# Graph attention layer on one core: the transposed node one-hots are compared by GpSimd instead of turned on TensorE

## The reference

```python
feats = jnp.maximum(x @ w1 + bb1, 0.0) @ w2 + bb2
x_cat = jnp.concatenate([feats[row], feats[col], elem[:, None]], axis=1)
hid = jnp.maximum(x_cat @ a1 + aab1, 0.0)
e1 = (hid @ a2 + aab2)[:, 0]
e1 = jax.nn.leaky_relu(e1, negative_slope=0.2)
w = jnp.exp(e1 - jnp.max(e1))
pooled = jax.ops.segment_sum(w[:, None] * feats[col], row, num_segments=n)
row_sum = jax.ops.segment_sum(w, row, num_segments=n) + 1e-10
return pooled / row_sum[:, None]
```

## Time and profile before

| what | value |
|---|---|
| time, median of 3 executions | 4831.8 us (4830.55 to 4842.57) |
| profiled execution, span from its first to its last instruction | 4828.3 us |
| busy, share of the span | TensorE 88%, VectorE 92%, ScalarE 79%, GpSimd 56% |
| tile loop | from about 1556 us to about 4690 us |

### The profile page before, as it was taken

One profiled execution on the slowest core, in us unless ns is written; L12 is line 12 of the kernel. 1 busy time (PEld: TensorE's weight loads), 2 busy tenths in 40 slices (PEclk: granted clock), 3 DMA queues, 4 the chain that ended last, 5 costly groups with the idle time before them and its releaser, 6 DMA issues.

```text
span 4828.3 us, 133194 instructions
## 1 busy us (share of the span) xinstructions
PE 4260.4 (88%) x24114; PEld 3004.1 (62%) x24115; DVE 4460.2 (92%) x25378; ACT 3835.5 (79%) x12983; POOL 2693.5 (56%) x2886
## 2 busy tenths in 40 slices
PE   1598998898896999999999999999999999999990
PEld 1355555555555777777777777777777777777760
DVE  8799999999996999999999999999999999999998
ACT  1587778778774888888888888888888888888884
POOL 5366666666664555555555555555555555555544
PEclk9999999999997999999999999999999999999995
DMA  2133333333334877777777777777777777777757
GB/s 85 43 73 86 79 71 80 81 77 80 79 76 137 240 225 221 228 225 224 224 225 224 225 225 221 226 224 224 225 224 224 224 225 225 225 225 225 221 172 212
DMA packets 266918, 851.82 MB, mean 176 GB/s; under 512 B 107916, under 2 KB 109584, under 8 KB 266861
## 3 DMA queue, kind: packets, MB, share of 16 engines
q0 software_dynamic: 169920, 673.54, 50.0%
q1 hardware_dynamic: 63543, 160.18, 11.2%
q10 hardware_dynamic: 33398, 17.49, 1.4%
HBM read 739.10 MB, written 111.90 MB: 176 GB/s over the span
## 4 chain that ended last, share of the span: by engine, by line
PE 36%; ACT 27%; issue 3%; DVE 2%; DMA 1%; ACTq 0%; POOL 0%; DVEq 0%; SPq 0%; POOLq 0%
ACT z L1164 18%; PE psum L971 15%; PE psum L975 9%; PE psum L958 8%; ACT onehot L1193 3%; ACT onehot_t L1182 3%; PE psum L984 3%; ACT onehot L1197 2%; PE psum L939 1%; DVE z L1689 1%; DVE z L1682 0%; PE psum L995 0%; ACT onehot L1195 0%; DVE z L1705 0%; DMA p_win<-p_table 0%
## 5 line engine op out<-in xcount | busy, mean ns | idle before, releaser
L754 POOL DMA_INDIRECT z<-qf_table,rec x1664 | 1609.2, 967 | 1454.9 <-PE psum L958 1027.1
L1164 ACT ACTIVATE z<-z 128x64 f32<-128x64 f32 x6656 | 1651.1, 335 | 0.0
L971 PE MATMUL psum<-p_win,onehot_t 128*128 x9984 | 1407.8, 274 | 84.1 <-ACT onehot_t L1182 68.3
L971 PEld LDWEIGHTS psum<-p_win,onehot_t 128*128 128x128 bf16 x9984 | 966.8, 97 | 540.0 <-issue 214.4
L958 PE MATMUL psum<-z,onehot 128*128 128x260 f32 x3328 | 1029.4, 391 | 6.7 <-DVE acc L1617 4.9
L975 PE MATMUL psum<-z,ident 128*128 128x258 f32 x3328 | 1002.7, 383 | 0.0
L1568 DVE SCALAR_TENSOR_TENSOR z<-z,a_b 128x129 f32<-128x129 f32 x3328 | 884.3, 290 | 5.6 <-issue 0.2
L1568 DVE SCALAR_TENSOR_TENSOR z<-psum,a_b 128x129 f32<-128x129 f32 x3328 | 828.2, 286 | 0.0
L1558 DVE TENSOR_TENSOR z<-z,psum 128x258 f32<-128x258 f32 x1664 | 698.6, 420 | 94.6 <-PE psum L975 90.6
L1617 DVE TENSOR_TENSOR acc<-acc,psum 125x260 f32 x1664 | 702.3, 422 | 25.3 <-PE psum L958 2.4
L695 POOL DMA_INDIRECT sorted_rows<-z x300 | 478.5, 1595 | 403.9 <-DVE z L1447 321.6
(11 more groups left out here) (220 smaller groups left out, 5576.3 us busy)
## 6 DMA issues: line engine op xcount, KB each, us to landing
p_table<-acc SPq DMA_DIRECT2D x100, 338.6 KB
p_win<-p_table SPq DMA_DIRECT2D x100, 338.6 KB
z<-qf_table,rec POOLq DMA_INDIRECT x1664, 4.5
qf_table<-acc SPq DMA_DIRECT2D x75, 339.5 KB
acc<-in_x_dram SPq DMA_DIRECT2D x25, 448.0 KB
z<-in_x_dram SPq DMA_DIRECT2D x20, 560.0 KB
out_dram<-z ACTq DMA_DIRECT2D x20, 560.0 KB
qf_table<-z SPq DMA_DIRECT2D x25, 339.5 KB
```

Source lines behind the costliest of these rows:

```text
L754: pool.indirect_dma_start(out=z_t[:, o + j, :], out_offset=None, in_=qf_table, in_offset=bass.IndirectOffsetOnAxis(ap=rec[:, o + j, 3:4].b ...
L971: mm = pe.matmul(to, onehot_t[:, j, :], p_flat[:, bass.ds((w % 2) * (3 * ZW) + (part * ZW + o), n)], start=(part == 0), stop=(part == 2 an ...
L1164: op = act.activation(z_t[:, slot, o:o + DO], z_t[:, slot, o:o + DO], ACT.Copy, scale=z_t[:, slot, o + DO:o + HF])
```

## The change

The transposed one-hots no longer come from the others. In the stage that makes the records, GpSimd also takes the row numbers and the three weight parts of each group as bf16 (`rows_b`), and SyncE writes them to `edge_rows` in device memory. In the tile loop ScalarE starts three transfers for each group of four tiles (`load_nodes`): the 512 row numbers go to all of partitions 0 to 124 (as 112 and 13 partitions), and the three weight parts to partitions 125 to 127 of `onehot_t`, which now has three halves. GpSimd then compares 125 x 512 of them in place with each partition's number (`match_nodes`). `turn`, `take_turned` and the copy of the weight parts are gone. ScalarE makes the f32 one-hots, which only `sum_up` still reads, a step later. Some semaphores are merged, and two constants move in SBUF.

```diff
+    HALVES = 3
...
+        node_id = sb("node_id", [P, 1])
-        onehot_t = sb("onehot_t", [P, SB, P], BF16)
+        onehot_t = sb("onehot_t", [P, HALVES, SB // 2, P], BF16)
...
             for g in range(BULK):
+                sp.wait_ge(s_rows_b, g + 1)
+                sp.dma_start(rows_t[g * P:(g + 1) * P, :, :], rows_b[:, g % 2, :, :]).then_inc(s_rows_st[g % 2], 16)
                 sp.wait_ge(s_field_a, g + 1)
...
+            for g in range(BULK):
+                pool.wait_ge(s_stage[g % 4], g // 4 * 16 + 16)
+                if g >= 2:
+                    pool.wait_ge(s_rows_st[g % 2], g // 2 * 16)
+                of = stage[:, g % 4, :].rearrange("p (s f) -> p f s", f=NF)
+                pool.tensor_copy(rows_b[:, g % 2, 0, :], of[:, 0, :])
+                pool.tensor_copy(rows_b[:, g % 2, 1:4, :], of[:, 3:6, :]).then_inc(s_rows_b, 1)
...
+                def match_nodes(off, u):
+
+                    h = (k + off) * 2 + u
+                    pool.wait_ge(s_oht_ld[h % HALVES], (i * 2 + h // HALVES) * 48 + 48)
+                    pool.sem_inc(s_passed, 1)
+                    own = onehot_t[0:WN, h % HALVES, :, :].rearrange("p t n -> p (t n)")
+                    pool.tensor_scalar(own, own, node_id[0:WN, :], None, ALU.is_equal).then_inc(s_oht, 1)
+
                 for j in range(SB):
                     if live(i, k, 1):
                         gather(j)
+                    if j == 1 and live(i, k, 0):
+                        match_nodes(0, 1)
+                    if j == 5 and live(i, k, 1):
+                        match_nodes(1, 0)
...
-                def turn(off, u):
-
-                    group = (i * SPB + (k + off)) * 2 + u
-                    pe.wait_ge(s_onehot, group + 1)
-                    since(pe, s_oht, group)
-                    for j in range(HALF_SB):
-                        mm = pe.transpose(psum[:, 6, j * P:(j + 1) * P], onehot[:, ((k + off) * SB + u * HALF_SB + j) % RING, :], ident[:, :])
-                    mm.then_inc(s_oht_mm, 1)
...
-                    act.activation(onehot_t[:, u * HALF_SB:(u + 1) * HALF_SB, :].rearrange("p t n -> p (t n)"),
-                                   psum[:, 6, 0:HALF_SB * P], ACT.Copy).then_inc(s_oht, 1)
...
-                    act.activation(onehot[:, oo:oo + HALF_SB, WN:P], rec_b[:, oo:oo + HALF_SB, 2:5], ACT.Copy)
...
+                def load_nodes(off, u):
+
+                    h = (k + off) * 2 + u
+                    own = onehot_t[:, h % HALVES, :, :].rearrange("p t n -> p (t n)")
+                    at = bass.ds((i * SPB + (k + off)) * (SB * P) + u * (HALF_SB * P), HALF_SB * P)
+                    if live(i, k, off - 2 + u):
+                        act.wait_ge(s_z_mm, tile(off - 2 + u, (1 - u) * HALF_SB + HALF_SB - 1) + 2)
+                    for a, b in ROWS:
+                        act.dma_start(own[a:b, :], edge_rows[0:1, at].to_broadcast([b - a, HALF_SB * P])).then_inc(s_oht_ld[h % HALVES], 16)
+                    act.dma_start(own[WN:P, :], edge_rows[1:4, at]).then_inc(s_oht_ld[h % HALVES], 16)
...
+                if live(i, k, 1):
+                    load_nodes(1, 0)
                 if live(i, k, 0):
-                    take_turned(0, 1)
-                if live(i, k, 1):
-                    onehots(1, 0)
+                    onehots(0, 0)
...
-                    if j == 0 and live(i, k, 1):
-                        take_turned(1, 0)
                     if j == SB // 2 and live(i, k, 1):
-                        onehots(1, 1)
+                        load_nodes(1, 1)
+                    if j == SB // 2 and live(i, k, 0):
+                        onehots(0, 1)
```

More of the change, by code:

```diff
@@ L85, in gnn_layer @@
     records = nc.dram_tensor("records", (P * NT, 4), F32, kind="Internal").ap()
+    edge_rows = nc.dram_tensor("edge_rows", (4, NT * P), BF16, kind="Internal").ap()
     base_rows_d = nc.dram_tensor("base_rows", (BLOCKS, 2, CB * W), BF16, kind="Internal").ap()
@@ L324, in gnn_layer @@
         s_onehot = sem("s_onehot")
-        s_oht_mm = sem("s_oht_mm")
+        s_rows_b = sem("s_rows_b")
+        s_rows_st = [sem(f"s_rows_st{n}") for n in range(2)]
+        s_oht_ld = [sem(f"s_oht_ld{n}") for n in range(HALVES)]
         s_oht = sem("s_oht")
@@ L580, in _ @@
             sp.wait_ge(s_rec_st, 16 * BULK)
+            for n in range(2):
+                sp.wait_ge(s_rows_st[n], (BULK + 1 - n) // 2 * 16)
             sp.dma_start(rec[:, 0:SB, :].rearrange("p t n -> p (t n)"), rec_d[:, 0:SB * 4]).then_inc(s_rec[0], 16)
@@ L970, in hidden_src @@
                         for part in range(3):
[L971 removed]
+                            mm = pe.matmul(to, onehot_t[:, (k * 2 + j // HALF_SB) % HALVES, j % HALF_SB, :], p_flat[:, bass.ds((w % 2) * (3 * ZW) + (part * ZW + o), n)],
                                            start=(part == 0), stop=(part == 2 and not (o and PEH)), skip_group_check=True)
@@ L1005, in step @@
                         hidden_src(j)
-                    if j == SB // 4 and live(i, k, 0):
-                        turn(0, 1)
                     if j == SB // 4 and live(i, k, -1):
@@ L1011, in step @@
                         max_to_all()
-                    if j == SB - SB // 4 and live(i, k, 1):
-                        turn(1, 0)
                     if j % 4 == 3 and j < SB - 1 and live(i, k, 0):
```

86 lines of the change are left out of this document (40 added, 46 removed).

## The result

The changed kernel takes 4928.15 us in the median of four executions (4925.22 to 4934.23), the kernel before 4831.18 (4830.36 to 4842.57). The ratio is 1.0198, with an interval of 1.0184 to 1.0213: slower by 97 us, where 73 us less was forecast. The profiled execution of the changed kernel has a span of 4932.4 us and was the slowest of the four (4934.23 as timed).

What follows compares the result with a forecast made beforehand. TensorE bounds now, VectorE after the change: 14.28 + 0.43 = 14.71 us a step, 0.38 less; 208 x 0.38 = 79, less 6, is 73 us faster: 4759 from the median, range 4680 to 4950.

Steps and rivals of the forecast that it cites:

- M: Time of one GpSimd compare of 125 x 512: 0.87 us taken, 0.62 at the least, 2.50 at the most.
- GpSimd's own time does not matter: GpSimd's queue in the tile loop: 8.2 us a step plus 1.7, said not to matter; only the effect on VectorE would.
- TensorE stops being the bound: Tile loop: TensorE falls to 13.98 us at most, VectorE's 14.13 plus 0.15 idle gives 14.28 a step without new cost.
- break-even of 1.15: Compare length in us above which holding VectorE eats the 0.78 us gain left after the start's 6 us.
- VectorE held until GpSimd's instruction is done: Tile loop: the skill's exclusive port lock holds VectorE's two-SBUF-input products for GpSimd's whole instruction; price 0.43 us a step.
- the rival that had this M (1.6): VectorE held longer than it gains, in tiles 1 and 6: 1.68 us, 15.96 a step, 5019; 27 in 100.
- Where the compares fall: Compares miss VectorE's products for 1.08 us behind the sixth gather (no cost), 0.44 behind the second (price 0.43 us).
- my 4.24 us: Time from the start of tile j - 2 to the compare behind gather j: 0.76 + 1.10 + 1.42 + 0.96.
- ScalarE 13.7 us a step: ScalarE: 12.88 less 1.17 plus 2.0 for six transfer starts; rival that it becomes the bound, 4834, 10 in 100.
- the DMA: Rival: row numbers land late and the compare holds gathers; half a microsecond a step gives 4863; 5 in 100.
- Once, +6 us: Outside the steps: 1 us for record-stage casts and stores, about 5 us later first TensorE product at the loop's start.
- The sign: Whole kernel: faster 0.58, same 0.12, slower 0.30 (the held VectorE, the DMA and the rest).

Runs made afterwards that it cites:

- experiment 7: The changed kernel with each compare cut to 256 of its 512 columns, same queue places, the other columns left uncompared: 4770.98 us, 0.9877.
- experiment 3: The kernel before, nothing removed, plus two GpSimd compares of 125 x 512 a step on a scratch tile that nobody waits for: 4843.03 us, 1.0025.

## Why the prediction was wrong, point by point

Two steps of the prediction failed: the size of the compare M, and the sentence that GpSimd's own time does not matter. A third, the length of the hold, erred the other way and hid part of the other two.

- **TensorE stops being the bound, 14.28 us a step without new cost.** Right in kind, 0.27 low: with the 4-column compare the step is 14.55. VectorE's busy time came out as said (384.64 / 400 x 14.55 = 13.99, said 14.13) and the wait for `head_max` went. But the addition's wait for TensorE stayed at 0.30 us (49.4 / 165) of the 0.40, and I had kept 0.15 for all idle time where 0.56 was left.
- **The compare, 0.87 us.** This is the term that failed first: 1.58 us undisturbed, 1.77 in the mean. With a compare of 1.09 us in the same places (experiment 7) the time is 4771, inside the forecast's 4720 to 4800, so this size alone turns the sign. It was inside my bounds (0.62 to 2.50) and above my own break-even of 1.15. I took 1.40 times a dense cast because the slow row was strided. The strided row scaled to 512 columns (2.50) was as near as the cast, and the figure of the Trainium skill (GPSIMD Engine Reference, side-by-side cycle accounting), 769 ns for a tight loop over 512 elements, is half of the 1.58 us measured here.
- **VectorE held until GpSimd's instruction is done.** Wrong in length: until 0.85 us into 1.58, where the rule of the Trainium skill named above gives 1.58. VectorE's instructions grow by some 0.65 us a step ((309 - 289) x 16 = 0.32 and 0.33 for `max_diag`), not by the 1.68 of the rival that had this M (1.6). That rival's 5019 is only 91 us too high because it knew nothing of the waits that come on top; the closeness is luck.
- **Where the compares fall: 1.08 us free behind the sixth gather, 0.44 behind the second.** Wrong in both. By the middle values of 2000 to 2600 us they start 0.39 us into tile 6 and 1.06 into tile 1, where I had worked out 1.20 into tile 5 and 0.32 into tile 1: both some 0.7 us late. It is the same with the 4-column compare, so the hold is not the reason; which term of my 4.24 us is short I did not separate. In the timeline above the compare behind the sixth gather meets a product after 0.09 us; the one behind the second meets a product under way and `max_diag`, an SBUF operation that I had not listed.
- **"GpSimd's own time does not matter."** The missed term, put at nothing. It is true of the gathers behind the compare (experiment 3, at most 12 us). It is not true of the compare, which is itself part of GpSimd's queue, behind a gather and its pauses, and a tile or two ahead of TensorE's need: 107 to 127 us where the products are not held, 17 on top of the hold. I had asked only what stands behind the compare, not what stands ahead of it and how soon its result is wanted.
- **ScalarE 13.7 us a step.** Its busy time, in which the profile does not count the starts of transfers, is 308.02 / 400 x 15.48 = 11.9. The starts, for which I had added 2.0, lie beside running activations: a start of 0.33 us at 3004.83 falls into multiplications that go on from 3003.77 to 3007.47. This rival is out. So is the DMA: the share is 0.78, and the profile puts 1.3 us in 2400 of GpSimd's idle time ahead of gathers down to the loads.
- **Once, +6 us.** The wait at the loop's start was right (6.2 us, said 5). Ahead of the loop I allowed 1 us. In the ten other variants of the changed kernel the first gather comes at 1561.55 to 1563.88 us, in the kernel before at 1556.48 and in experiment 3 at 1556.23. So the change costs 5 to 7 us there; the 2 to 4 more in the changed kernel's own profile are that execution's, since the variants' programs are the same up to there. Which of the new casts and stores it is was not tried.
- **The sign.** The chance of slower was 0.30, on the condition "M over 1.15", and this condition was met. Its reason, VectorE held for the whole instruction, was not what happened: the hold is shorter, and waits that the prediction did not have came on top. The right sign of the rival is in part luck.

The best versions are the changed kernel with its compares two places earlier, 4799 us, cut in two at the early places, 4801, or on VectorE, 4804: 0.6 to 0.7% faster than before, and not to be told apart by their intervals. About 62 us lie between that and the 4737 of a compare that takes almost no time. A start of the compare timed to miss VectorE's SBUF products was not tried.

## What to carry to other kernels

When work moves to an engine with idle time, its price is the place in that engine's queue: ask what stands ahead of it, how long that can stall at the worst, and how soon the result is wanted, and put it early enough to cover the worst pause. When GpSimd is that engine, look as well at which VectorE operation with only SBUF operands is under way when its instruction starts or lies beside its first microsecond. And where a cost is known only to within a factor of four, and the sign turns inside that factor, the forecast should stand on the sign's break-even, not on a likely middle.

## What the runs showed of the hardware that I had not expected

- A compare of 125 x 512 in bf16 takes 1.58 us on GpSimd and 0.38 on VectorE; undisturbed, 256 columns take 0.94 and 4 columns 0.31 (in the mean of their runs 1.09 and 0.45). A compare of 512 that begins while a product of VectorE with both inputs in SBUF is under way takes up to 1.97, as at 3015.15 (the product ran from 3015.02 to 3015.34).
- The hold is partial. In the changed kernel, products that begin 0.35 to 0.38 us into a compare of 1.58 us end at 0.85 (24 between 2000 and 2600 us), and those that begin 0.56 to 0.86 us into it run in 0.28 (52). With 256 columns the end is at 0.64 of 0.94 us. An iota holds `max_diag` to its own end and the products not at all. In the compare of 1.97 us at 3015.15 a product that begins 0.33 us into it is not held, and `max_diag`, 0.54 us into it, is held until 1.10. Why the window lies where it does, no run here shows. The additions and products with a PSUM input were not longer than before (413 and 281 ns, before 420 and 286).
- GpSimd's issue of gathers pauses for 2.3 to 3.8 us. The distance goes with the gathers and not with time: 169.8 us in the mean in the kernel before, 174.3 in the changed one, 163.7 with the 4-column compare, which is 11.25 steps or 90 gathers in each. What they are, no run here shows.
